# Graph attention on one core: which partitions the two load queues fill when they share a load of the adjacency matrix

## The chip, the cores and the metric

The kernel runs on one core of a Trainium2 chip. The metric is the device time of one execution in microseconds (us), lower is better. Transfers are issued on two queues, one fed by the SyncE sequencer (SP) and one by ScalarE (ACT), and both run on the core's 16 DMA engines.

## The reference

`x` is 4096 x 128, `adj` 4096 x 4096 of int32 with 0 or 1. What is computed:

```
h  = max(layernorm(x), 0)
Wh = h @ W
e  = leaky_relu((Wh @ a1)[:, None] + (Wh @ a2)[None, :], slope 0.2)
e  = where(adj > 0, e, -9e15)
out = x + elu(softmax(e, axis=1) @ Wh)
```

The matrix `adj` is 67.1 MB and is read once; everything else is small.

## The kernel before

The 4096 output rows are worked through in four chunks `c` of 1024 rows. A chunk is made of 8 units `u`, each of 512 columns of `adj`, so that a unit is 1024 rows x 512 columns, 2.1 MB of int32. For a unit ScalarE turns the int32 values to bytes in two activations of 128x2048 elements, TensorE transposes the bytes (16 transposes, line 1017), VectorE multiplies them with the attention weights (line 815, four instructions for a unit, tile `words`), and TensorE multiplies the words with the values (lines 1041 to 1043, tile `acc`).

`adj` comes in 32 loads of 2.1 MB, written out in a table, `LOADS`, and numbered 0 to 31. They land in a ring of four slots, `raw`:

- Loads 0 to 9 are single units; each row of 512 columns is one run of 2 KB. SP fetches both halves (`h is None` below).
- Loads 10 to 19 and 28 to 31 are halves of two neighbouring units: four rows of 1024 columns to each partition, with runs of 4 KB. The text calls these pair loads; `two_to_bytes` (line 554) converts them. In the code they are the entries with a pair of units, and the views `raw_two` and `rows_of_two` belong to them.
- Loads 20 to 27 are sets. They serve the units 4 to 7 of chunks 2 and 3 and come with another layout, in four quarters of 32 partitions each, with runs of 2 KB. VectorE transposes them (line 795, `turn_set`), and `set_to_bytes` (line 572) converts them.

Up to load 11 SP fetches alone (`SHARED` is 12). From load 12 on both queues fetch a part of 1.05 MB each. Of a set SP takes the quarters 0 and 1, that is partitions 0 to 63, and ACT takes 64 to 127. Of a pair load, each queue takes two of the four rows of every one of the 128 partitions. ACT issues its part right after its conversion of the load four before:

```
if at < SHARED: SP alone, k = 0 and 1
SP : raw_two[at % RING][:, 0:2]   <- rows 0, 1 of each partition, to semaphore raw_in[slot][0]
ACT: raw_two[at % RING][:, 2:BT]  <- rows 2, 3 of each partition, to semaphore raw_in[slot][1]
```

The order on each engine is written out by hand. Both queues wait on `act_bytes` until load `at - 4` has been converted. A conversion of a pair load waits for both `raw_in` semaphores of its slot, and of a unit for one per half. Chunk 3 works its units in the order 4, 0, 5, 1, 6, 2, 7, 3: unit 4 wants the sets up to load 27, and unit 0 the pair loads 28 and 29.

Of the kernel before, what the change touches and what calls it, by code (L numbers as in the profile page):

```python
# [16 lines left out]
P = 128  # L17
BT = 4
# [18 lines left out]
RING = 4  # L37
# [5 lines left out]
def bass_graph_attention(nc: bass.Bass, x: bass.AP, adj: bass.AP, w: bass.AP, a: bass.AP, out: bass.AP):  # L43
# [10 lines left out]
    LOADS = [(0, u, None) for u in range(U)] + [(1, u, None) for u in range(2)]  # L54
# [3 lines left out]
    SHARED = U + RING  # L58
# [24 lines left out]
    with ExitStack() as ctx:  # L83
# [6 lines left out]
        def sem(name):  # L90
            return ctx.enter_context(nc.semaphore(name))
# [84 lines left out]
        raw_two = [raw[:, s].rearrange("p (t w) j -> p t (w j)", w=2) for s in range(RING)]  # L176
# [21 lines left out]
        def rows_of(c):  # L198

            if c < SETS:  # L200
                return x_sb[:, group(c)]
            t0 = T * VP // 2 + (c - SETS) * CHUNK
            return val_f32[:, t0:t0 + CHUNK].rearrange("p (t f) -> p t f", f=F)

        def is_set(c, u):
            return c >= SETS and u >= 4
# [14 lines left out]
        def rows_of_two(c, units, h):  # L221

            return (adj_two if c < SETS else adj_two_lin)[c, h, units[0] // 2]
# [6 lines left out]
        raw_in = [[sem(f"raw_in{s}_{k}") for k in range(2)] for s in range(RING)]  # L230
# [76 lines left out]
        gen_out = sem("gen_out")  # L307
        GEN_STEPS = 10
        OUT_DMAS = C - 1 + 3
        SP_QUARTERS, ACT_QUARTERS = (0, 1), (2, 3)  # L310
        MOVES = 4 * 4

        block = ctx.enter_context(nc.Block())
# [8 lines left out]
        @block.sync  # L322
        def _(sp):
            def load_x(b):
                sp.dma_start(x_sb[:, b * BT:(b + 1) * BT, :], x_v[b]).then_inc(x_in[b], 16)

            def load_raw(at, k):
                c, u, h = LOADS[at]
                if h is None:
                    sp.dma_start(raw[:, at % RING, k * BT:(k + 1) * BT], adj_v[c, k, u]).then_inc(raw_in[at % RING][k], 16)  # L330
                else:
                    sp.dma_start(raw_two[at % RING][:, 2 * k:2 * k + 2], rows_of_two(c, u, h)[:, 2 * k:2 * k + 2]).then_inc(raw_in[at % RING][k], 16)

            def load_set(at):

                c, _, h = LOADS[at]
                for k in SP_QUARTERS:
                    sp.dma_start(raw[k * QUARTER:(k + 1) * QUARTER, at % RING], adj_set[c, 1, h, k]).then_inc(set_in[at % RING], 16)

            def load_rows(c):  # L340
                sp.dma_start(rows_of(c).rearrange("p t f -> p (t f)"), x_lin[c]).then_inc(rows_in[c], 16)

            for b in range(4):
                load_x(b)
            load_raw(0, 0)
            for b in range(4, 6):
                load_x(b)
            load_raw(0, 1)
            for b in range(6, NB):
                load_x(b)  # L350
            for at in range(1, C * U):

                if LOADS[at][1] is None:
                    sp.wait_ge(act_bytes, 2 * (at - RING) + 1)
                    load_set(at)
                else:
                    for k in range(2 if at < SHARED else 1):
                        if (at, k) == (RING, 0):
                            sp.wait_ge(first_bytes, 1)
                        elif at >= RING:  # L360
                            sp.wait_ge(act_bytes, 2 * (at - RING) + (k if LOADS[at][2] is None else 1))
                        load_raw(at, k)

            sp.wait_ge(words_free, SETS * U * BT)
            sp.wait_ge(val_moved, MOVES)
            load_rows(C - 2)
            load_rows(C - 1)

            last = out_lin[C - 1].rearrange("p (t f) -> p t f", f=F)
            for k, (t0, t1) in enumerate(BANKS):  # L370
                sp.wait_ge(last_res, k + 1)
                sp.dma_start(last[:, t0:t1], rows_of(C - 1)[:, t0:t1]).then_inc(out_done, 16)

            sp.wait_ge(general_ready, 1)
            with sp.If(sp.value_load(general[0:1, 0:1], min_val=0, max_val=1) > 0):
                sp.wait_ge(out_done, 16 * OUT_DMAS)
                with sp.Fori(0, NB) as b:
                    with sp.Fori(0, BT) as q:
                        sp.wait_ge(gen_res, b * BT + q + 1)
                        sp.nop(nofuse=True)  # L380
                        sp.dma_start(adj_rows, adj_rows_v[bass.ds(b, 1), :, bass.ds(q, 1)].rearrange("g p q j -> (g p q) j")
                                     ).then_inc(gen_in, 16)
                        sp.dma_start(x_tile, x_v[bass.ds(b, 1), :, bass.ds(q, 1)].rearrange("g p q f -> (g p q) f")
                                     ).then_inc(gen_in, 16)
                        sp.wait_ge(gen_res, b * BT + q + 2)
                        sp.nop(nofuse=True)
                        sp.dma_start(out_rows_v[bass.ds(b, 1), :, bass.ds(q, 1)].rearrange("g p q f -> (g p q) f"), res_tile
                                     ).then_inc(gen_out, 16)
                        sp.wait_ge(gen_out, (b * BT + q + 1) * 16)
                        sp.nop(nofuse=True)  # L390

            sp.wait_ge(out_done, 16 * OUT_DMAS)

        @block.gpsimd
        def _(pool):
# [76 lines left out]
            def move_values():  # L472
# [6 lines left out]
                for k in range(4):  # L479
                    for m in range(4):  # L480

                        if moves:
# [3 lines left out]
                                              val_u[m * QUARTER:(m + 1) * QUARTER, (4 + k) * BT:(5 + k) * BT]).then_inc(val_moved, 1)  # L486
                pool.wait_ge(val_moved, MOVES)

# [10 lines left out]
        def _(act):  # L499
# [76 lines left out]
            def load_half(at):  # L576

                if SHARED <= at < C * U:
                    c, u, h = LOADS[at]
                    act.wait_ge(act_bytes, 2 * (at - RING) + 1)  # L580
                    if u is None:
                        for k in ACT_QUARTERS:
                            act.dma_start(raw[k * QUARTER:(k + 1) * QUARTER, at % RING], adj_set[c, 1, h, k]).then_inc(set_in[at % RING], 16)  # L583
                    else:
                        act.dma_start(raw_two[at % RING][:, 2:BT], rows_of_two(c, u, h)[:, 2:BT]).then_inc(raw_in[at % RING][1], 16)

            def row_copy(g, k):
                act.wait_ge(spread_ps, 2 * g + k + 1)
# [8 lines left out]
            def square(g):  # L597

                if g == 0:
                    act.wait_ge(vh_ready, 2 + G - 1)  # L600
                    act.wait_ge(val_moved, MOVES)
                else:
# [58 lines left out]
            for at in range(U, C * U):  # L661
                c, u, h = LOADS[at]
                if u is None:
                    set_to_bytes(c, h)
                elif h is None:
                    for k in range(2):
                        if at == U:
                            row_copy(G - 1, k)
                        to_bytes(c, u, k)
                else:  # L670
                    two_to_bytes(at)
                load_half(at + RING)
                if at == 13:
                    tail(0)
                if at == 27:
                    tail(1)
# [34 lines left out]
        def _(dve):  # L711
# [86 lines left out]
            def weights(c, i, q):  # L798

                n, u = c * U + i, ORDER[c][i]  # L800
                if q == 0:
                    if is_set(c, u):
                        dve.wait_ge(set_turned, (c - SETS) * 4 + u - 4 + 1)
                        dve.wait_ge(val_moved, MOVES)
                    else:
# [165 lines left out]
        def _(pe):  # L971
# [49 lines left out]
            def value_tile(c, i, q):  # L1021
                u = ORDER[c][i]
                return val_set[:, (u - 4) * BT + q] if is_set(c, u) else val[:, u * BT + q]

            def product(c, i, q):
# [3 lines left out]
                if is_set(c, ORDER[c][i]):  # L1029
                    pe.wait_ge(val_moved, MOVES)  # L1030
                v = value_tile(c, i, q)
# [172 lines left out]
```

## Time and profile before

| what | value |
|---|---|
| time, median of 3 runs | 238.54 us (238.23 to 240.66) |
| the profiled execution | 238.26 us, with a span of 236.4 us in the trace and 1.86 us around it |
| TensorE (PE) matmul busy | 218.4 us, 92% of the span |
| VectorE (DVE) busy | 198.7 us, 84% |
| ScalarE (ACT) busy | 158.2 us, 67% |
| GpSimd (POOL) busy | 81.0 us, 34% |
| read from memory | 70.32 MB, 306 GB/s over the span |
| granted TensorE clock | 0.996 of full speed |

The chain of work that ended last is made up of PE for 35% of the span, DMA for 33% and ACT for 17%. Shares of busy time are averages; which engine limits a stretch has to be read stretch by stretch.

### The profile page before, as it was taken

The numbers are of one execution on the slowest core, as the hardware profiler recorded it, in microseconds if no ns is written. First come the engines' busy times: TensorE is split into PE (matmuls) and PEld (weight loads), VectorE is DVE, ScalarE is ACT, GpSimd is POOL, SyncE is SP. The second block draws the span as 40 slices with busy tenths as digits, with TensorE's granted clock in tenths as the row PEclk, the third lists the DMA queues.
The fourth block names the chain that finished last, engine by engine and source line by source line (L and its number), as shares of the span: only waits on it lengthen the run. The fifth ranks groups of instructions, "written<-read, shape, count | busy, mean of one in ns | idle before, by whom it ended". The sixth has DMA issues, their size and how long they took to land.

```text
span 236.4 us, 8053 instructions
## 1 busy us (share of the span) xinstructions
PE 218.4 (92%) x3608; PEld 212.4 (90%) x3608; DVE 198.7 (84%) x266; ACT 158.2 (67%) x139; POOL 81.0 (34%) x68
## 2 busy tenths in 40 slices
PE   6968899999999999999999999999995699999990
PEld 1757899999999999999999999999994699999980
DVE  3999989766669988877787987999989499989866
ACT  3698999966778388977776666666287819920033
POOL 4648127799000110799700300000009700791000
PEclk9999999999999999999999999999999999999998
DMA  6999999999999999999999999999999814010002
GB/s 219 343 392 387 386 386 384 386 385 386 394 408 409 407 409 407 407 411 403 295 316 366 366 362 365 363 362 307 327 407 407 345 70 180 3 79 15 3 0 90
DMA packets 29622, 72.93 MB, mean 308 GB/s; under 512 B 1554, under 2 KB 2068, under 8 KB 29588
## 3 DMA queue, kind: packets, MB, share of 16 engines
q1 hardware_dynamic: 21136, 49.81, 57.6%
q10 hardware_dynamic: 8452, 22.61, 26.4%
q8 instruction: 28, 0.46, 0.8%
q14 instruction: 6, 0.05, 0.1%
HBM read 70.32 MB, written 2.10 MB: 306 GB/s over the span
## 4 chain that ended last, share of the span: by engine, by line
PE 35%; DMA 33%; ACT 17%; DVE 8%; issue 3%; ACTq 2%; DVEq 0%
DMA raw<-in_adj_dram 32%; ACT mask L554 11%; PE acc L1041 10%; PE acc L1043 10%; PE acc L1042 10%; PE mask_t L1017 4%; DVE stats L730 3%; DMA first<-in_x_dram 1%; ACTq L583 1%; PE acc L1005 1%; ACT neg L694 1%; ACT mask L543 1%; DVE wh_sb L756 1%; PE acc L996 1%; ACT second L572 1%
## 5 line engine op out<-in xcount | busy, mean ns | idle before, releaser
L815 DVE SCALAR_TENSOR_TENSOR words<-g_row,gq_word,mask_t 128x1024 f32<-128x1024 f32 x96 | 119.7, 1275 | 27.6 <-PE mask_t L1017 14.7
L1042 PE MATMUL acc<-val,words 128*128 128x129 f16 x744 | 128.0, 220 | 0.0
L1043 PE MATMUL acc<-val,words 128*128 128x129 f16 x744 | 128.0, 220 | 0.0
L1041 PE MATMUL acc<-val,words 128*128 128x129 f16 x744 | 128.0, 220 | 0.0
L1041 PEld LDWEIGHTS acc<-val,words 128*128 128x128 f16 x744 | 72.8, 98 | 0.1
L1042 PEld LDWEIGHTS acc<-val,words 128*128 128x128 f16 x744 | 72.8, 98 | 0.1
L1043 PEld LDWEIGHTS acc<-val,words 128*128 128x128 f16 x744 | 72.8, 98 | 0.0
L554 ACT ACTIVATE mask<-raw,step_bias 128x2048 uint8<-128x2048 int32 x28 | 54.5, 1995 | 19.9 <-DMA raw<-in_adj_dram 7.2
L1041 PE MATMUL acc<-first,words 128*128 128x129 f16 x256 | 43.9, 220 | 2.2 <-DVE num L823 1.6
L1043 PE MATMUL acc<-first,words 128*128 128x129 f16 x256 | 43.9, 220 | 0.0
L1042 PE MATMUL acc<-first,words 128*128 128x129 f16 x256 | 43.9, 220 | 0.0
L815 DVE SCALAR_TENSOR_TENSOR words<-g_row,first,mask_t 128x1024 f32<-128x1024 f32 x32 | 38.7, 1270 | 0.0
L543 ACT ACTIVATE mask<-raw,step_bias 128x2048 uint8<-128x2048 int32 x19 | 37.4, 1997 | 0.6 <-ACT mask L543 0.6
L462 POOL TENSOR_SCALAR hp<-hp 128x1024 f32<-128x1024 f32 x3 | 10.9, 3633 | 69.9 <-ACT neg L649 69.9
L1017 PE MATMUL mask_t<-ident_b,mask 128*128 128x128 bf16 x384 | 25.4, 219 | 3.0 <-ACT mask L554 3.0
L1041 PEld LDWEIGHTS acc<-first,words 128*128 128x128 f16 x256 | 25.0, 98 | 2.5 <-DVE words L815 2.5
L1017 PEld LDWEIGHTS mask_t<-ident_b,mask 128*128 128x128 bf16 x384 | 22.5, 98 | 3.2 <-ACT mask L554 3.1
L1042 PEld LDWEIGHTS acc<-first,words 128*128 128x128 f16 x256 | 25.1, 98 | 0.0
L1043 PEld LDWEIGHTS acc<-first,words 128*128 128x128 f16 x256 | 25.1, 98 | 0.0
L572 ACT ACTIVATE second<-raw,step_bias 128x2048 uint8<-128x2048 int32 x8 | 15.6, 1995 | 7.3 <-DMA raw<-in_adj_dram 7.3
L458 POOL TENSOR_TENSOR hp<-num,rz 128x1024 f32<-128x1024 f32 x3 | 5.7, 1898 | 38.2 <-DVE rz L826 38.1
L572 ACT ACTIVATE g_row<-raw,step_bias 128x2048 uint8<-128x2048 int32 x4 | 8.0, 2004 | 10.2 <-DMA raw<-in_adj_dram 10.2
(113 smaller groups left out, 219.1 us busy)
## 6 DMA issues: line engine op xcount, KB each, us to landing
raw<-in_adj_dram SPq DMA_DIRECT2D x36, 1024.0 KB, 14.6
raw<-in_adj_dram ACTq DMA_DIRECT2D x12, 1024.0 KB, 11.7
raw<-in_adj_dram SPq DMA_DIRECT2D x16, 512.0 KB, 12.4
raw<-in_adj_dram ACTq DMA_DIRECT2D x16, 512.0 KB, 15.6
first<-in_x_dram SPq DMA_DIRECT2D x8, 256.0 KB, 6.5
val<-in_x_dram SPq DMA_DIRECT2D x2, 512.0 KB, 17.0
out_dram<-first ACTq DMA_DIRECT2D x2, 512.0 KB, 3.3
out_dram<-val ACTq DMA_DIRECT2D x1, 512.0 KB, 2.6
```

The source lines that it names most:

```text
L458: nc.gpsimd.tensor_tensor(hp[:], num[:, :, 0:F], rz[:].unsqueeze(2).broadcast_to([P, CT, F]), ALU.mult).then_inc(hp_ready, 1)
L462: nc.gpsimd.tensor_scalar(hp[:], hp[:], 0.0, -1.0, ALU.max, ALU.add).then_inc(pos_ready, 1)
L543: nc.scalar.activation(mask[:, mask_slot(c, u), k * BT:(k + 1) * BT], raw[:, at % RING, k * BT:(k + 1) * BT], ACT.Sign, scale=1.0, bias=st ...
L554: nc.scalar.activation(mask[:, mask_slot(c, u), h * BT:(h + 1) * BT], raw_two[at % RING][:, :, i * BLOCK:(i + 1) * BLOCK], ACT.Sign, scale ...
L572: nc.scalar.activation(pair_bytes[PAIRS[c][k]][:, :, h], raw[:, at % RING, :, k * 256:(k + 1) * 256].rearrange("p t (m x) -> p m t x", m=2 ...
L583: act.dma_start(raw[k * QUARTER:(k + 1) * QUARTER, at % RING], adj_set[c, 1, h, k]).then_inc(set_in[at % RING], 16)
L730: last = nc.vector.bn_stats(stats[:, t, :], x_sb[:, t, :])
L815: nc.vector.scalar_tensor_tensor(words[:, q], g_row[:, c * CHUNK:(c + 1) * CHUNK], word, bytes_t, ALU.max, ALU.mult).then_inc(words_ready, 1)
L1017: last = nc.tensor.transpose(maskt_pairs[:, i % 2, h, t * P:(t + 1) * P], mask_pairs[:, mask_slot(c, u), t, :, h], ident_b[:])
L1041: nc.tensor.matmul(acc_tile(t), high, v[:, 0, 0:V], start=first and t % PT == 0, stop=False, skip_group_check=True)
L1042: nc.tensor.matmul(acc_tile(t), high, v[:, 1, 0:V], start=False, stop=False, skip_group_check=True)
L1043: last = nc.tensor.matmul(acc_tile(t), low, v[:, 0, 0:V], start=False, stop=False, skip_group_check=True)
```

## The change

SP and ACT no longer split a pair load by rows but by partitions, as they do with sets. SP fetches all four rows of partitions 0 to 63, and ACT all four rows of partitions 64 to 127. This holds for the shared pair loads, 12 to 19 and 28 to 31. Loads 10 and 11, which SP fetches alone, stay in two transfers of 128 partitions each. Bytes per transfer, run length, the order of issue, waits and semaphores stay as they are.

```diff
+        SP_HALF, ACT_HALF = slice(0, P // 2), slice(P // 2, P)
...
+            def load_two(at):
+
+                c, u, h = LOADS[at]
+                sp.dma_start(raw_two[at % RING][SP_HALF], rows_of_two(c, u, h)[SP_HALF]).then_inc(raw_in[at % RING][0], 16)
...
-                        load_raw(at, k)
+                        if at < SHARED:
+                            load_raw(at, k)
+                        else:
+                            load_two(at)
...
-                        act.dma_start(raw_two[at % RING][:, 2:BT], rows_of_two(c, u, h)[:, 2:BT]).then_inc(raw_in[at % RING][1], 16)
+                        act.dma_start(raw_two[at % RING][ACT_HALF], rows_of_two(c, u, h)[ACT_HALF]).then_inc(raw_in[at % RING][1], 16)
```

SP's queue from load 2 on, before. The names are the tile and the shape written (partitions x rows x columns); the twelve rows of line 332 are the loads 10 and 11 with two transfers each and 12 to 19 with one:

```order
L330 DMA raw<-in_adj_dram 128x4x512 [waits act_bytes] x11
L332 DMA raw<-in_adj_dram 128x2x1024 [waits act_bytes] x12
L338 DMA raw<-in_adj_dram 32x8x512 [waits act_bytes]
L338 DMA raw<-in_adj_dram 32x8x512
...
L332 DMA raw<-in_adj_dram 128x2x1024 [waits act_bytes] x4
L341 DMA val<-in_x_dram 128x1024 [waits val_moved,words_free]
```

The same place in the changed kernel:

```order
L332 DMA raw<-in_adj_dram 128x4x512 [waits act_bytes] x11
L334 DMA raw<-in_adj_dram 128x2x1024 [waits act_bytes] x4
L339 DMA raw<-in_adj_dram 64x4x1024 [waits act_bytes] x8
L345 DMA raw<-in_adj_dram 32x8x512 [waits act_bytes]
L345 DMA raw<-in_adj_dram 32x8x512
...
L339 DMA raw<-in_adj_dram 64x4x1024 [waits act_bytes] x4
L348 DMA val<-in_x_dram 128x1024 [waits val_moved,words_free]
```

Nothing changed places on SP. Four transfers stay as wide as they were, and twelve are now half as wide and twice as deep.

ACT's queue where the sharing begins, around its parts of loads 12 to 14, before:

```order
L543 ACTIVATE mask<-raw,step_bias 128x2048 [waits turned,raw_in0_1]
L585 DMA raw<-in_adj_dram 128x2x1024 [waits act_bytes]
L543 ACTIVATE mask<-raw,step_bias 128x2048 [waits turned,raw_in1_0]
L543 ACTIVATE mask<-raw,step_bias 128x2048 [waits turned,raw_in1_1]
L585 DMA raw<-in_adj_dram 128x2x1024 [waits act_bytes]
L554 ACTIVATE mask<-raw,step_bias 128x2048 [waits turned,raw_in2_1,raw_in2_0]
```

The same place in the changed kernel:

```order
L553 ACTIVATE mask<-raw,step_bias 128x2048 [waits turned,raw_in0_1]
L595 DMA raw<-in_adj_dram 64x4x1024 [waits act_bytes]
L553 ACTIVATE mask<-raw,step_bias 128x2048 [waits turned,raw_in1_0]
L553 ACTIVATE mask<-raw,step_bias 128x2048 [waits turned,raw_in1_1]
L595 DMA raw<-in_adj_dram 64x4x1024 [waits act_bytes]
L564 ACTIVATE mask<-raw,step_bias 128x2048 [waits turned,raw_in2_1,raw_in2_0]
```

Here too only the shape of the transfers differs. The first such transfer, load 12's part, is issued while SP's queue still holds a load of the old width.

## Rows read from the trace of the kernel before

**Rows 1.** The page: busy tenths of PE and DMA, and GB/s, in 40 slices of 5.9 us

```profile
PE   6968899999999999999999999999995699999990
...
DMA  6999999999999999999999999999999814010002
GB/s 219 343 392 387 386 386 384 386 385 386 394 408 409 407 409 407 407 411 403 295 316 366 366 362 365 363 362 307 327 407 407 345 70 180 3 79 15 3 0 90
```

**Rows 2.** Stretches of the span: us, busy of PE, PEld, DVE, ACT, POOL, clock, DMA share, GB/s

```profile
40.00:64.00 24.00, 24.00 (x409) 23.95 (x407) 16.10 (x14) 18.45 (x15) 16.23 (x10) 1.00 1.05 386
72.00:112.00 40.00, 40.00 (x709) 39.99 (x707) 34.51 (x33) 30.48 (x18) 16.87 (x14) 1.00 1.03 408
113.00:121.00 8.00, 8.00 (x145) 8.00 (x143) 5.56 (x6) 6.36 (x4) 3.90 (x6) 1.00 1.05 279
124.00:160.00 36.00, 36.00 (x640) 36.00 (x638) 32.31 (x30) 25.03 (x14) 1.90 (x1) 1.00 1.06 364
161.00:169.00 8.00, 8.00 (x145) 8.00 (x143) 8.00 (x8) 4.04 (x3) 0.00 (x0) 1.00 1.05 291
170.00:176.00 6.00, 6.00 (x109) 6.00 (x107) 5.14 (x5) 3.93 (x3) 0.00 (x0) 1.00 1.03 406
177.00:186.00 9.00, 3.88 (x64) 3.44 (x62) 6.10 (x8) 7.62 (x6) 8.64 (x4) 1.00 1.02 407
```

**Rows 3.** Waits of PE between 176 and 188 us: total, times, longest

```profile
PE mask_t L1017 <- ACT mask L554: 3.0, 1, 3.0
PE acc L1041 <- DVE num L823: 1.6, 1, 1.6
PE acc L1041 <- DVE words L815: 0.6, 1, 0.6
```

**Rows 4.** ACT in order of time, conversions and issues: start, us, what, idle before

```profile
68.52 0.47 ACTq L585 DMA_DIRECT2D raw<-in_adj_dram  x1
...
73.02 0.47 ACTq L585 DMA_DIRECT2D raw<-in_adj_dram  x1
...
81.09 3.90 ACT L554 ACTIVATE mask<-raw,step_bias 128x2048 uint8<-128x2048 int32 x2 [3.58 <-DMA raw<-in_adj_dram]
...
86.14 3.90 ACT L554 ACTIVATE mask<-raw,step_bias 128x2048 uint8<-128x2048 int32 x2 [1.15 <-DMA raw<-in_adj_dram]
...
128.66 3.90 ACT L572 ACTIVATE second<-raw,step_bias 128x2048 uint8<-128x2048 int32 x2 [1.87 <-DMA raw<-in_adj_dram]
...
134.36 3.90 ACT L572 ACTIVATE second<-raw,step_bias 128x2048 uint8<-128x2048 int32 x2 [1.81 <-DMA raw<-in_adj_dram]
...
145.77 3.90 ACT L572 ACTIVATE second<-raw,step_bias 128x2048 uint8<-128x2048 int32 x2 [1.82 <-DMA raw<-in_adj_dram]
...
163.35 2.00 ACT L572 ACTIVATE g_row<-raw,step_bias 128x2048 uint8<-128x2048 int32 x1 [2.21 <-DMA raw<-in_adj_dram]
...
171.53 2.00 ACT L572 ACTIVATE g_row<-raw,step_bias 128x2048 uint8<-128x2048 int32 x1 [4.28 <-DMA raw<-in_adj_dram]
...
183.25 3.90 ACT L554 ACTIVATE mask<-raw,step_bias 128x2048 uint8<-128x2048 int32 x2 [1.34 <-DMA raw<-in_adj_dram]
```

**Rows 5.** Line 585 between 68 and 69 us: the landing of its one transfer

```profile
DMA to landing us min/median/max: 10.9/10.9/10.9
```

**Rows 6.** DVE in order of time, around unit 4 of chunks 2 and 3

```profile
149.81 1.25 DVE L795 STREAM_TRANSPOSE mask_t<-second 128x1024 uint32<-128x1024 uint32 x1
...
169.80 4.85 DVE L815 SCALAR_TENSOR_TENSOR words<-g_row,first,mask_t 128x1024 f32<-128x1024 f32 x4
175.51 1.26 DVE L795 STREAM_TRANSPOSE mask_t<-g_row 128x1024 uint32<-128x1024 uint32 x1 [0.86 <-issue]
```

**Rows 7.** PE in order of time: the transposes of unit 2 of chunk 1 and of unit 0 of chunk 3

```profile
86.43 1.06 PE L1017 MATMUL mask_t<-ident_b,mask 128*128 128x128 bf16 x16
...
185.31 1.07 PE L1017 MATMUL mask_t<-ident_b,mask 128*128 128x128 bf16 x16 [2.96 <-ACT mask L554]
```

## The prediction

> **What bounds the kernel now.** I read the page's slices first [rows 1]. PE is busy in tenths of 9 from slice 5 to the end, but for two slices near 180 us, and the DMA engines are full from slice 1 to slice 30. So two things run side by side at their limits, and the question is where one waits for the other. The stretches [rows 2] say: PE is busy for the whole of each one up to 176 us and for only 3.88 of 9 us in 177 to 186. The waits of PE there [rows 3] are 3.0 us for a conversion of `mask`, 1.6 us for `num` and 0.6 us for `words`, 5.2 us in all.
>
> The 3.0 us wait ends with the transposes at 185.31 us [rows 7], those of unit 0 of chunk 3. They need the first activation of load 29. Load 29 is the one whose arrival ACT waited for at 183.25 [rows 4]; its two activations take 3.90, so the first ends near 185.25. Only loads 30 and 31 come after it, for units 2 and 3, several units of PE work later. The end of the kernel is therefore the time of these transposes plus a constant, and they have two fetters: the arrival of load 29 plus 2.0 us, and the point where PE itself is through with the work before them, 185.31 - 2.96 = 182.35 us.
>
> Now the loads. The other arrivals that ACT waited for [rows 4] are load 11 at 81.09, load 12 at 86.14, the sets 20, 21 and 23 at 128.66, 134.36 and 145.77, and the sets 26 and 27 at 163.35 and 171.53. Since the engines are full throughout, throughput lost anywhere between 68 and 183 us arrives as lateness of load 29, one to one. The stretches give the rates: units fetched by SP alone 386 GB/s, pair loads 408, sets 364, and two hollows of 8 us with 279 and 291 GB/s [rows 2]. The first hollow ends some 8 us before load 20 arrives, the first set, so it lies where pair loads spread over all partitions meet sets split by partition; the second lies where sets meet pair loads again.
>
> **A reading of the hollows.** If each half of the partitions can take half of the 408 GB/s, 204, then two queues whose bytes fall unevenly on the halves lose. SP spread over all 128 and ACT on 64 to 127 alone, with equal turns, put three quarters of the bytes on the upper half: 204 / 0.75 = 272 GB/s. The hollows have 279 and 291. Sets from both queues are even, and run at 364. The trace doesn't name partitions, so this is an inference; the nearness of 272 to 279 carries it. The Trainium skill (SBUF — State Buffer, section "Door 1: The DMA port swizzle") says the same from the other side: 64 neighbouring partitions reach only 8 of 16 ports. That agrees with the hollows' rates.
>
> **What the change does, part by part.**
>
> *Count of instructions and bytes.* Twelve transfers on each queue change shape; none is added, none moves, all keep 1.05 MB in runs of 4 KB. I cost the issue at nothing: 0.47 us on ACT [rows 4] before as after, and if it rose by a tenth of a microsecond, ACT's waits of 1 to 4 us before its conversions would hide it.
>
> *Edit 1, the start of the sharing: a new hollow.* ACT's part of load 12 is issued at 68.52 [rows 4] and lands 10.9 us later [rows 5], at 79.4, while SP still delivers load 11, 128 partitions wide, until 81.09. Before, the two were alike in width, and no hollow shows (408 in 72 to 112). After, ACT writes the upper half alone beside SP's full width: the pattern of the hollows. At their mean, 285 GB/s, SP's share is 142. How much of SP's wide data lies in the overlap? ACT's part needs 1.05 MB / 204 = 5.1 us, so it began between 68.5 and 74.3, and SP moved for 6.8 to 12.6 us beside it, that is 1.39 to 2.57 MB. I take the 2.1 MB of load 11. At 204 it needs 10.3 us, at 142 it needs 14.8: load 11 is **4.5 us late**, at 85.6; from the bounds 3.0 to 5.5. ACT's parts of 12 and 13 meanwhile run ahead, which gives nothing back: from here SP's parts end each load, and SP can no longer take the whole machine when ACT's queue is empty, since it reaches one half only.
>
> *Edit 2, pair loads 12 to 19 split by partition.* Each needs 1.05 MB of SP. At 204 GB/s that is 5.14 us. The only row with two queues split this way is that of the sets, 364 against 386 for the same 2 KB runs in full width, a factor of 0.94; by it 204 becomes 192, and a load takes 5.46. I take 5.4, close to the row of the same pattern. Eight loads: 43.2 us, to 128.8.
>
> *Edit 3, the two old hollows go.* Pair loads and sets now have the same halves on the same queues. So load 20, a set, follows after its 5.70 us (134.36 - 128.66): at 134.5, **5.8 us later** than the 128.66 of before. Bounds: 84.1 + 8 x 5.14 + 5.7 = 130.9 and 86.6 + 8 x 5.46 + 5.7 = 136.0, late by 2.2 and 7.3. Load 23 stays 17.1 behind load 20, as before: 151.6. Load 27 is 7 x 5.7 = 39.9 behind: 174.4, against 171.53, because the second hollow (8.18 instead of 5.7 us between 26 and 27) is gone. Load 29 is two pair loads on: 185.2, against 183.25, **1.95 us late**.
>
> *The transposes at 185.31.* By load 29: 185.2 + 2.0 = 187.2. By PE's own path: VectorE starts on load 23 at 149.81 with no idle time ahead [rows 6], 0.14 us after its conversion ends (145.77 + 3.90), so its 5.8 us of lateness go straight into VectorE, which then works with little pause (4 words of 1.21 us and a transpose of 1.26 a unit, 8.00 of 8 busy in 161 to 169 [rows 2]) to the transpose at 175.51, where it has 0.86 us idle to give. Load 27's conversion would end at 178.3, which comes before VectorE at 174.65 + 5.8 = 180.45. So PE is ready at 182.35 + 5.8 - 0.86 = 187.3. ACT's own chain, 174.4 + 3.90, two activations of 1.06 with a gap of 0.54, and 3.90 for load 28, ends at 184.9, before load 29. Both paths say 187.3 instead of 185.3: **2.0 us**.
>
> *Where cover could fail.* The lateness of load 11 also meets PE: its transposes at 86.43 [rows 7] need the first activation of load 11, now at 85.6 + 2.0 = 87.6. PE stalls about 1.2 us there. This costs nothing at the end, as PE then waits less at 182 to 187.
>
> **The sum.** Profiled execution: 238.26 = 236.4 + 1.86. With 2.0 more in the span, 238.4 + 1.86 = 240.3 us. The medians of the runs shown lie 0.3 above the profiled execution, which I leave in the range. By the bounds: low, load 29 at 84.1 + 41.1 + 5.7 + 39.9 + 10.3 = 181.1 and PE ready at 182.35 + 2.2 - 0.86 = 183.7, so 1.6 us faster, 236.7; high, PE ready at 188.8 and load 29 at 186.8, so 3.5 slower, 241.8.
>
> **The rivals.**
>
> *A, the old hollows stay as well.* The cause of a hollow may be the switch of the engines from one kind of load to the other, some ahead of others, whichever queue fills which half. For it: the second hollow lasts 8 us, though only four loads are in flight. Then the new hollow is added to two old ones. Each costs 8 us x (386 - 285) GB/s = 0.81 MB, 2.1 us. Load 29 comes at 185.2 + 4.2 = 189.4, the transposes at 191.4: 244.4 us. It decides from the point where load 29's first activation passes PE's own 187.3, so any remainder of a hollow over 0.1 us shows.
>
> *B, no new hollow.* If full width beside the upper half costs nothing when both have 4 KB runs (the hollows mix 4 and 2 KB), load 11 keeps its 81.09, and the old hollows go. Load 29 then comes at 178.1 to 180.7, and PE is ready at 181.5 to 182.8. That is 2.5 to 3.8 us faster: 234.5 to 235.8. Against it: 272 fits the hollows without the run lengths, and the step from 2 to 4 KB runs on SP alone, at 64 to 72 us in the slices, shows no hollow [rows 1].
>
> *C, nothing.* The change does not do what it says for the traffic: engines and turns mix so that width doesn't matter, hollows stay, none is added. 238.3, give or take 0.7.
>
> *D, the halves serialise.* If two half-width transfers took turns, each pair load would need 2.1 MB / 204 = 10.3 us instead of 5.15; ten such loads up to load 29 make 51 us, 289 us. The sets, split this way, run at 364 [rows 2], which is nearly a disproof. The Trainium skill (SBUF — State Buffer, "Can I just issue two DMAs to hit both halves?") holds that two such transfers serialise and gain 6% together; this trace disagrees at 364 GB/s.
>
> **How the numbers follow.** Chances: forecast 0.45, A 0.20, B 0.15, C 0.17, D 0.03. A difference of 1% (236.2 to 240.9) is about what a measurement of this kernel can tell. Faster by over 1%: B and a little of the forecast's low end, 0.17. Within 1%: C and somewhat over half of the forecast, 0.40. Slower: the rest of the forecast, A and D, 0.43. The range takes in the forecast's bounds, C and A, whose own spread ends at 245; it leaves out B below 236.5 and D, together 0.18.
>
> **What would show it.** Right: a hollow of 270 to 300 GB/s between 71 and 87 us; load 11 converted at 85 to 86 instead of 81; a PE stall of about 1 us at its transposes; a flat rate through 112 to 124 and 160 to 169; sets shifted by about 5.8 us; a PE wait near 185 of under 1 us for `mask`. Wrong: 408 GB/s held through 71 to 87 (B); 280 at both old places (A or C); PE waiting at new places in chunk 1 for more than 3 us.

## The result and the profile after

The changed kernel takes 254.71 us (median of 4 runs, 252.16 to 256.29), against 239.34 us for the kernel before beside it. The ratio is 1.060, with a 95% interval of 1.049 to 1.072: slower, and by far more than the forecast of 240.3 us. Medians here take in every run, while ratios and intervals leave out slow ones, over 1.5% above the fastest run of the same kernel. The profiled execution took 252.16 us, with a span of 250.4 us, 14.0 us longer than before.

The page's slices after, answering [rows 1]; here 40 slices of 6.3 us:

```profile
PE   6967999999999999999999995199994499999990
...
PEclk9999999999999999999999999569999889999996
...
GB/s 209 356 389 387 387 386 384 386 385 388 404 346 268 325 334 332 329 336 341 332 310 362 366 365 368 362 361 350 316 323 299 284 158 203 41 3 86 3 0 85
```

PE now has two holes instead of one, and the granted clock falls in or behind both. The rate has a plateau of 325 to 341 GB/s where the pair loads 12 to 19 run, the place that had 408. Stretches of the kernel after, answering [rows 2]; the columns are the same:

```profile
72.00:80.00 8.00, 8.00 (x143) 7.99 (x140) 7.48 (x8) 4.74 (x3) 0.00 (x0) 1.00 1.04 273
88.00:112.00 24.00, 24.00 (x428) 24.00 (x426) 19.52 (x16) 17.59 (x10) 11.02 (x7) 1.00 1.03 332
113.00:121.00 8.00, 8.00 (x145) 8.00 (x143) 5.60 (x5) 3.90 (x2) 7.33 (x11) 1.00 1.03 333
124.00:132.00 8.00, 8.00 (x146) 8.00 (x144) 6.74 (x9) 5.21 (x3) 0.00 (x0) 1.00 1.04 314
136.00:160.00 24.00, 17.72 (x314) 17.54 (x310) 11.94 (x10) 16.29 (x9) 0.00 (x0) 0.94 1.05 365
173.00:181.00 8.00, 8.00 (x145) 8.00 (x143) 8.00 (x8) 3.62 (x2) 0.00 (x0) 1.00 1.03 317
```

The new hollow of 273 GB/s at 72 to 80 us is there, as predicted. Behind it the reader should see what was not predicted: 332 GB/s, steady, for pair loads split by partition. The two old hollows are shallower but still there, later than before: 314 GB/s from 124 to 132 us, behind the issue of the first set's parts at 119.15, and 317 from 173 to 181. The sets run at 365 as before. ACT in order of time, answering [rows 4]:

```profile
82.44 3.90 ACT L564 ACTIVATE mask<-raw,step_bias 128x2048 uint8<-128x2048 int32 x2 [4.99 <-DMA raw<-in_adj_dram]
...
88.55 3.90 ACT L564 ACTIVATE mask<-raw,step_bias 128x2048 uint8<-128x2048 int32 x2 [2.21 <-DMA raw<-in_adj_dram]
...
132.81 3.90 ACT L564 ACTIVATE mask<-raw,step_bias 128x2048 uint8<-128x2048 int32 x2 [1.64 <-DMA raw<-in_adj_dram]
...
138.35 3.90 ACT L582 ACTIVATE second<-raw,step_bias 128x2048 uint8<-128x2048 int32 x2 [1.64 <-DMA raw<-in_adj_dram]
...
155.31 3.89 ACT L582 ACTIVATE second<-raw,step_bias 128x2048 uint8<-128x2048 int32 x2 [1.64 <-DMA raw<-in_adj_dram]
...
172.72 2.00 ACT L582 ACTIVATE g_row<-raw,step_bias 128x2048 uint8<-128x2048 int32 x1 [1.91 <-DMA raw<-in_adj_dram]
...
182.26 2.00 ACT L582 ACTIVATE g_row<-raw,step_bias 128x2048 uint8<-128x2048 int32 x1 [5.64 <-DMA raw<-in_adj_dram]
...
195.57 3.90 ACT L564 ACTIVATE mask<-raw,step_bias 128x2048 uint8<-128x2048 int32 x2 [2.77 <-DMA raw<-in_adj_dram]
```

These are the arrivals of loads 11, 12, 19, 20, 23, 26, 27 and 29. Against [rows 4] the lateness is 1.4 us at load 11, 2.4 at 12, 9.7 at 20, 9.5 at 23, 10.7 at 27 and 12.3 at 29. PE's waits between 148 and 205 us, answering [rows 3], the VectorE row behind the longest, answering [rows 6], and the transposes that wait for load 29, answering [rows 7]:

```profile
PE acc L1051 <- DVE words L825: 8.6, 2, 8.0
PE mask_t L1027 <- ACT mask L564: 4.5, 1, 4.5
PE acc L1051 <- DVE num L833: 1.7, 1, 1.7
```

```profile
159.24 1.26 DVE L805 STREAM_TRANSPOSE mask_t<-second 128x1024 uint32<-128x1024 uint32 x1 [9.64 <-ACT second L582]
```

```profile
197.62 0.56 PE L1027 MATMUL mask_t<-ident_b,mask 128*128 128x128 bf16 x7 [4.55 <-ACT mask L564]
```

The first hole of PE is load 23: its conversion ends at 155.31 + 3.89 = 159.2, VectorE transposes at 159.24 after 9.64 us idle, and PE waits 8.0 us for the words. This wait does not set the end, since PE has to wait for load 29 again. The transposes at 197.62 are 12.3 us later than the 185.31 of before, and the span is 14.0 us longer. The other 1.7 us lie right behind them. The next unit's transposes, before and after, are already 13.95 us apart:

```profile
194.37 1.06 PE L1017 MATMUL mask_t<-ident_b,mask 128*128 128x128 bf16 x16
```

```profile
208.32 1.06 PE L1027 MATMUL mask_t<-ident_b,mask 128*128 128x128 bf16 x16
```

Between the two units the clock was granted at 0.79 from 196 to 204 us, after PE had been idle.

The granted clock (the last column but two) in stretches behind the two holes:

```profile
160.00:164.00 4.00, 2.30 (x22) 2.30 (x23) 4.00 (x5) 2.87 (x2) 0.00 (x0) 0.50 1.06 361
164.00:168.00 4.00, 4.00 (x43) 4.00 (x41) 4.00 (x5) 2.12 (x2) 0.00 (x0) 0.55 1.06 366
168.00:172.00 4.00, 4.00 (x75) 4.00 (x72) 3.87 (x4) 2.81 (x2) 0.00 (x0) 1.00 1.06 361
...
196.00:204.00 8.00, 6.38 (x84) 6.38 (x85) 4.90 (x5) 4.61 (x3) 2.40 (x2) 0.79 0.96 231
```

At 0.55 PE gets through 43 matmuls in 4 us, at 1.00 through 75.

### The profile page after: what moved, and what is told of

Read it like the earlier page. It is cut to its first block, busy times and chain, and to the rows that moved or that the text cites. A ratio compares the mean times of both kernels' runs of the same rounds, so it can differ in the third digit from the quotient of the medians.

```text
span 250.4 us, 8053 instructions
## 1 busy us (share of the span) xinstructions
PE 223.4 (89%) x3608; PEld 217.2 (87%) x3608; DVE 199.1 (80%) x266; ACT 158.2 (63%) x139; POOL 81.1 (32%) x68
## 4 chain that ended last, share of the span: by engine, by line
DMA 36%; PE 34%; ACT 15%; DVE 7%; issue 4%; ACTq 3%; DVEq 0%
DMA raw<-in_adj_dram 35%; PE acc L1051 9%; PE acc L1053 9%; PE acc L1052 9%; ACT mask L564 7%; PE mask_t L1027 4%; DVE stats L740 3%; ACTq L593 2%; ACT mask L553 2%; ACT second L582 2%; DMA first<-in_x_dram 1%; PE acc L1015 1%; ACT neg L704 1%; DVE wh_sb L766 1%; PE acc L1006 1%
## 5 line engine op out<-in xcount | busy, mean ns | idle before, releaser
L1051 PE MATMUL acc<-first,words 128*128 128x129 f16 x256 | 46.7, 227 | 2.2 <-DVE num L833 1.7
L1052 PE MATMUL acc<-first,words 128*128 128x129 f16 x256 | 46.6, 227 | 0.0
L1053 PE MATMUL acc<-first,words 128*128 128x129 f16 x256 | 46.5, 227 | 0.0
L1051 PEld LDWEIGHTS acc<-first,words 128*128 128x128 f16 x256 | 26.1, 102 | 2.6 <-DVE words L825 2.6
L1052 PEld LDWEIGHTS acc<-first,words 128*128 128x128 f16 x256 | 26.1, 102 | 0.0
L1053 PEld LDWEIGHTS acc<-first,words 128*128 128x128 f16 x256 | 26.0, 102 | 0.0
```

The lines of the kernel that those rows point to most:

```text
L1051: nc.tensor.matmul(acc_tile(t), high, v[:, 0, 0:V], start=first and t % PT == 0, stop=False, skip_group_check=True)
L1052: nc.tensor.matmul(acc_tile(t), high, v[:, 1, 0:V], start=False, stop=False, skip_group_check=True)
L1053: last = nc.tensor.matmul(acc_tile(t), low, v[:, 0, 0:V], start=False, stop=False, skip_group_check=True)
```

## The experiments

Each kernel was timed beside the kernel before on the same chip. Most cuts of code leave out the semaphore calls, and where both queues change alike they show one. Rates and arrivals are read from one profiled run of each kernel.

**Source or destination?** The change alters two things in a transfer: which partitions it writes, and which rows it reads. The two queues now read rows megabytes apart. Two kernels take them apart; theory D says that the destination counts (it is not the prediction's rival D), theory S the source. The first keeps full width and reads far apart:

```diff
+    adj_far = adj.rearrange("(c b s p q) (w j) -> c b w s p q j", b=2, s=2, p=P, q=2, j=2 * BLOCK)
-    act.dma_start(raw_two[at % RING][:, 2:BT], rows_of_two(c, u, h)[:, 2:BT])
+    act.dma_start(raw_two[at % RING][:, 2:BT], far(c, u, h, 1))      # SP: far(c, u, h, 0)
```

> The kernel before, with each queue's part of a shared pair load still written over all 128 partitions, but read from two blocks of rows that lie as far apart as in the changed kernel (SP the first half of the rows of a load, ACT the second). Rows so land in other places than the reference wants. Theory D (destination: the halves of the partitions and what they share sets the rate): pair loads stay at 400 to 410 GB/s, time 238 to 240 us. Theory S (source: two far streams of rows clash in memory): pair loads fall to about 333 GB/s as in the changed kernel, time 250 to 255 us.

Measured: ratio 0.995 (0.990 to 0.999), median 238.06 us. Its stretch from 88 to 112 us:

```profile
88.00:112.00 24.00, 24.00 (x428) 24.00 (x426) 19.24 (x16) 19.00 (x11) 17.31 (x16) 1.00 1.03 409
```

409 GB/s: distance in memory costs nothing. The second keeps the halves and reads close together:

```diff
+    adj_near = adj.rearrange("(c b i a s q) (w j) -> c b w s i a q j", b=2, i=P // 2, a=2, s=2, q=2, j=2 * BLOCK)
-    act.dma_start(raw_two[at % RING][ACT_HALF], rows_of_two(c, u, h)[ACT_HALF])
+    act.dma_start(raw_two[at % RING][ACT_HALF].rearrange("p (a q) j -> p a q j", a=2), near(c, u, h, 1))
```

> The changed kernel, with the partitions split 0 to 63 and 64 to 127 as in it, but each queue reads the rows that it read before (two of every four), so the two streams are neighbours in memory again. Rows so land in other places than the reference wants. Theory D: pair loads stay at about 333 GB/s, a hollow of about 270 between 72 and 80 us, time 252 to 256 us. Theory S: 385 to 408 GB/s outside the hollow, time 238 to 242 us.

Measured: ratio 1.059 (1.050 to 1.067), median 253.89 us, the whole slowdown. From 88 to 112 us:

```profile
88.00:112.00 24.00, 24.00 (x428) 24.00 (x426) 18.99 (x15) 16.88 (x11) 8.94 (x4) 1.00 1.03 338
```

The destination decides. Theory S is out.

**Form of the transfer or length of the runs?** Sets also go to halves and yet run at 364. They differ from the changed pair loads in two ways: 32 partitions per transfer, and runs of 2 KB. One kernel takes over each:

```diff
-    sp.dma_start(raw_two[at % RING][SP_HALF], rows_of_two(c, u, h)[SP_HALF])
+    for part in (slice(0, 32), slice(32, 64)):                       # ACT: 64 to 96, 96 to 128
+        sp.dma_start(raw_two[at % RING][part], rows_of_two(c, u, h)[part])
```

> The changed kernel with each queue's part in two transfers of 32 partitions (SP 0 to 31, 32 to 63; ACT 64 to 95, 96 to 127), as sets have them, still in 4 KB runs. If it is the 64-partition form of one transfer that costs the rate, it rises to the sets' 364 GB/s, time 243 to 246 us. If it is the 4 KB runs into a half, or the halves as such, it stays near 333, time 252 to 256 us.

Measured: ratio 1.057 (1.051 to 1.063), median 252.63 us.

```profile
88.00:112.00 24.00, 24.00 (x428) 24.00 (x426) 19.24 (x16) 17.25 (x10) 10.77 (x7) 1.00 1.03 316
```

Quarters in 4 KB runs are no better, 316 GB/s. Now the runs:

```diff
-    sp.dma_start(raw_two[at % RING][SP_HALF], rows_of_two(c, u, h)[SP_HALF])
+    for part in ((SP_HALF, slice(None), slice(0, BLOCK)), (SP_HALF, slice(None), slice(BLOCK, 2 * BLOCK))):
+        sp.dma_start(raw_two[at % RING][part], rows_of_two(c, u, h)[part])      # ACT likewise
```

> The changed kernel with each queue's part in two transfers of 64 partitions x 4 rows x 512 columns, so in 2 KB runs as the sets have. If long runs cost more when two engines want one half, the rate rises to about 364 GB/s, time 243 to 246 us. If the form of 64 partitions sets it, it stays near 333 or falls, by the 0.94 between 386 and 408, to about 315, time 252 to 258 us.

Measured: ratio 1.016 (1.006 to 1.027), median 244.65 us. Stretches of this kernel:

```profile
72.00:80.00 8.00, 8.00 (x143) 7.99 (x141) 7.48 (x8) 6.32 (x4) 0.00 (x0) 1.00 1.05 279
...
88.00:112.00 24.00, 24.00 (x428) 24.00 (x426) 19.25 (x16) 17.27 (x11) 11.84 (x8) 1.00 1.05 361
112.00:124.00 12.00, 12.00 (x216) 12.00 (x214) 9.39 (x9) 8.36 (x5) 7.98 (x12) 1.00 1.05 367
...
160.00:176.00 16.00, 16.00 (x266) 16.00 (x265) 16.00 (x15) 10.12 (x6) 0.00 (x0) 0.93 1.06 355
```

Halving the runs lifts the rate from 332 to 361 GB/s, the sets' own (the quarters are as many transfers, so their number is not it), and both old hollows are gone: the rate stays at 355 to 367 in the stretches from 88 to 176 us. In full width the order is the other way round, 386 with 2 KB runs and 408 with 4 KB [rows 2]. The 386 are SP alone; but SP alone with 4 KB runs moved 411 GB/s from 64 to 68 us of the changed kernel, so that the number of queues does not explain it. The new hollow at 72 to 80, 279 GB/s, stays, for SP's load 11 is still full width beside ACT's upper half.

**Is it the halves, or only that a transfer has 64 partitions?** SP takes the even partitions, ACT the odd ones:

```diff
-        SP_HALF, ACT_HALF = slice(0, P // 2), slice(P // 2, P)
+        SP_HALF, ACT_HALF = slice(0, P, 2), slice(1, P, 2)
```

> The changed kernel with SP taking the even partitions of a shared pair load and ACT the odd ones, so that each queue's part reaches both the lower and the upper 64. Theory D (what counts is which of the lower and upper 64 a queue writes): no hollow at 72 to 80 us, pair loads at 400 to 408 GB/s, old hollows of 280 back at 112 to 120 and 160 to 168, time 238 to 240 us. Rival (fewer partitions in a transfer are slow wherever they lie): 333 GB/s, 252 us.

Measured: ratio 1.002 (0.995 to 1.008), median 239.73 us.

```profile
72.00:80.00 8.00, 8.00 (x142) 7.99 (x140) 7.48 (x8) 6.41 (x4) 0.00 (x0) 1.00 1.03 408
88.00:112.00 24.00, 24.00 (x428) 24.00 (x426) 19.27 (x16) 19.13 (x11) 16.54 (x15) 1.00 1.02 407
113.00:121.00 8.00, 8.00 (x145) 8.00 (x143) 5.56 (x6) 5.18 (x3) 2.35 (x4) 1.00 1.04 273
...
161.00:169.00 8.00, 7.99 (x142) 7.81 (x140) 8.00 (x8) 3.90 (x2) 0.00 (x0) 1.00 1.05 280
```

It behaves like the kernel before in every stretch, the two old hollows included, with 64 partitions, four rows deep, and 4 KB runs in each transfer, as in the changed kernel. So what counts is whether a transfer reaches both the lower and the upper 64.

**The halves tested the other way.** The kernel before, with both queues on the same half in the sets:

```diff
-        SP_QUARTERS, ACT_QUARTERS = (0, 1), (2, 3)
+        SP_QUARTERS, ACT_QUARTERS = (0, 2), (1, 3)
```

> The kernel before with another deal of the sets' quarters: SP 0 and 2, ACT 1 and 3, so both queues write the lower 64 partitions at first and the upper 64 after. Theory D (a half takes about half of the full rate): sets fall from 364 GB/s to between 204 and 300, depending on how far the queues run apart; at 250 the eight sets take 67 us in place of 46, so 20 us more, about 258 us. If halves don't matter: 364 GB/s and 238 us.

Measured: ratio 1.074 (1.057 to 1.091), median 255.67 us.

```profile
124.00:160.00 36.00, 30.81 (x535) 30.13 (x532) 23.50 (x22) 18.58 (x10) 1.90 (x1) 1.00 1.06 257
```

The sets fall from 364 to 257 GB/s. And the changed kernel with everything on SP's queue, lower half, then upper half:

```diff
                 sp.dma_start(raw_two[at % RING][SP_HALF], rows_of_two(c, u, h)[SP_HALF]).then_inc(raw_in[at % RING][0], 16)
+                sp.dma_start(raw_two[at % RING][ACT_HALF], rows_of_two(c, u, h)[ACT_HALF]).then_inc(raw_in[at % RING][1], 16)
-                        act.dma_start(raw_two[at % RING][ACT_HALF], ...)
```

> The changed kernel with ACT's part of each shared pair load issued on SP's queue too, behind SP's own (lower 64, then upper 64, 4 KB runs); ACT issues none of them, sets are as before. If one half can take only half of the full rate, pair loads run at 200 to 220 GB/s and the time is about 290 us, 12 loads x 4.9 us more. If what costs at 333 GB/s is only the meeting of two queues, they run near 408 and the time is 238 to 241 us.

Measured: two runs, 284.64 and 292.04 us; the profile is that of the second.

```profile
88.00:160.00 72.00, 53.85 (x888) 52.79 (x885) 42.79 (x37) 29.39 (x16) 21.69 (x20) 0.95 1.03 219
```

219 GB/s over 72 us is what writing one half at a time gives. The queue itself is not the limit, as SP's 411 GB/s in full width shows. The Trainium skill (SBUF — State Buffer, section "Door 1: The DMA port swizzle") gives about 218 GB/s as the asymptote of partitions 0 to 63, and this row agrees. The same page of the Trainium skill, in "Can I just issue two DMAs to hit both halves?", says that two such transfers together gain 6% over one; the sets' 364 and the changed kernel's 332 GB/s, against 219, disagree with it.

**Which loads cost what.** Only the last four pair loads split, in 4 KB runs:

```diff
-                        if at < SHARED:
+                        if at < 28:
                             load_raw(at, k)
```

> The kernel before, with only the pair loads 28 to 31 split by partition; 12 to 19 stay full width. In the changed kernel load 27 came 9.5 us after load 26 and load 29 another 13.3 after that, where before it was 8.2 and 11.7. If the costs simply add, load 29 comes 2.9 us later than before, near 186.2, and the time is 241 to 242 us. If matched halves do away with the hollow there, as the prediction had it, load 29 comes 1.8 us earlier and the time is 236 to 238 us.

Measured: ratio 1.016 (1.005 to 1.028), median 242.69 us. Loads 27 and 29, and the stretch of the old hollow:

```profile
172.74 2.00 ACT L582 ACTIVATE g_row<-raw,step_bias 128x2048 uint8<-128x2048 int32 x1 [3.99 <-DMA raw<-in_adj_dram]
...
185.43 3.90 ACT L564 ACTIVATE mask<-raw,step_bias 128x2048 uint8<-128x2048 int32 x2 [2.15 <-DMA raw<-in_adj_dram]
```

```profile
161.00:169.00 8.00, 7.75 (x138) 7.58 (x135) 8.00 (x8) 5.62 (x3) 0.00 (x0) 1.00 1.05 340
170.00:176.00 6.00, 5.72 (x101) 5.55 (x99) 6.00 (x6) 3.27 (x2) 0.00 (x0) 1.00 1.03 337
```

The hollow is shallower, 340 in place of 291, but nothing climbs back to 406 behind it. Load 29 is 2.2 us late. Of these, 1.7 us are there at load 24 (153.13 us against 151.46), before the first split load is issued: kernels that are alike up to a load differ by up to 2.7 us in its arrival (load 11: 78.38 us in e6, 81.09 in the kernel before). From load 24 on, the split costs 0.5 us. The span is 5.0 us longer, and the clock accounts for most of the rest: behind PE's 3.9 us wait for load 29 it was granted at 0.50 from 188 to 192 us and at 0.84 to 196, with 40 and 63 matmuls where full clock has 75, which is about 2.5 us.

The counterpart splits only loads 12 to 19 (`at < SHARED or at >= 28` keeps the last four at full width):

> The changed kernel with only the pair loads 12 to 19 split by partition; 28 to 31 are full width again. If the two groups' costs add, the time is that of the changed kernel less what the last four cost alone (1.6%, 3.9 us): 249.5 to 251.5 us, with PE's long wait near 152 us unchanged. If the last four lose more only because the loads before them are late, it falls to 247 or below.

Measured: ratio 1.036 (1.029 to 1.042), median 248.34 us. 3.6% and 1.6% make 5.2%, against 6.0% for both together; with intervals of 0.7 to 1.2 points each that is no evidence against plain addition, nor proof of it. The time lies 1 us under the expected band and above the rival's 247, so this run did not decide between the two. Its profile shows PE's long wait again, 8.9 us, a hollow of 281 GB/s from 172 to 180 us where the full-width pair loads return, and load 29 at 195.30 us, as late as the 195.57 of the changed kernel. As about half of what e7 lost in its profile is the clock, the two ratios are in any case no plain sum of transfer times.

**A version from these findings.** Keep 12 to 19 at full width, where 4 KB runs reach 408; split only 28 to 31 by partition, and in 2 KB runs, so that they match the sets before them in both respects:

```diff
+    for j in (0, BLOCK):                                             # loads 28 to 31 only
+        sp.dma_start(raw_two[at % RING][SP_HALF, :, j:j + BLOCK], rows_of_two(c, u, h)[SP_HALF, :, j:j + BLOCK])
```

> The kernel before, with only the pair loads 28 to 31 split by partition, and each part in two transfers of 64 partitions x 4 rows x 512 columns (2 KB runs). Theory: a hollow needs a queue whose transfers spread over both halves beside one that does not, and long runs into halves are what costs the rest; with neither, the sets' rate runs on. 161 to 169 us at 355 to 360 GB/s in place of 291, load 27 near 169.3 in place of 171.5, load 29 12 to 13 us after it at 181.5 to 182.3 in place of 183.3: 0.5 to 1.5 us faster than before, 237 to 239 us. If the hollow there comes from the change of load kind as such, load 29 comes later than 184 and the time is 240 us or more.

Measured: ratio 0.988 (0.984 to 0.992), median 236.37 us, against 239.62 for the kernel before: faster than both, by a small margin over the kernel before, and under the 237 to 239 expected. Two stretches, the arrival of load 27, and PE's wait for load 29's conversion:

```profile
161.00:169.00 8.00, 7.72 (x137) 7.55 (x135) 8.00 (x8) 5.41 (x3) 0.00 (x0) 1.00 1.06 357
...
177.00:186.00 9.00, 6.13 (x103) 5.64 (x101) 7.19 (x9) 8.68 (x5) 8.76 (x4) 1.00 1.06 358
```

```profile
170.34 2.00 ACT L587 ACTIVATE g_row<-raw,step_bias 128x2048 uint8<-128x2048 int32 x1 [1.91 <-DMA raw<-in_adj_dram]
```

```profile
PE mask_t L1036 <- ACT mask L569: 1.5, 1, 1.5
```

The second hollow is gone, 357 in place of 291 GB/s. Load 27 is converted 17.5 us after load 24 (152.80), in place of 20.1, and load 29 (181.80) 29.0 us after it, in place of 31.8; and PE waits 1.5 us for `mask` in place of 3.0. The profiled spans differ by 1.4 us only, 235.0 against 236.4, the medians by 3.3. The granted clock of the runs beside it was 0.972 to 0.988 for the kernel before and 0.983 to 0.993 here, so a part of the gain may come from shorter waits leaving the clock up; no run takes the two apart.

## Why the prediction was wrong

**The frame held.** The engines are full from 68 us to load 29, lateness adds up to that load, and the end is load 29's first activation plus a constant: 12.3 of the 14.0 us are exactly that. The second path, load 23 through VectorE to PE, showed as well, as the 8.0 us hole. By the prediction's rule it makes PE ready at 182.35 + 9.5 - 0.86 = 191.0 us; it was ready at 197.62 - 4.55 = 193.1, the low clock behind the hole being the likely rest, still ahead of load 29.

**The step that failed is edit 2**, "Pair loads 12 to 19 split by partition". It took the sets' factor of 0.94 for the price of the split. The factor belongs to 2 KB runs (e4: 361 GB/s); with 4 KB runs it is 332 / 408 = 0.81. Eight loads take 132.81 - 82.44 = 50.4 us, 6.3 each, not 43.2. That is 7.2 us of the miss. The row was the only one with that pattern, but it differed in run length, and the prediction's upper bound rested on it too: 5.46 us a load was no bound at all. The sets' own rate, 364 GB/s, gives 5.8 us a load and 46.1 us for eight, close to e4's 47.2 (81.56 to 128.71); the remaining 4.3 us are the 4 KB runs. No row of before showed 4 KB runs into halves, and that gap should have widened the range.

**Edit 1, the new hollow**, was right in place and depth (273 GB/s against 285 taken), and e4 and e5 show its cause: it stays while SP is full width beside ACT's half, and goes when ACT's part reaches both halves. Its size at load 11 can't be judged by the two profiles of the sum, 82.44 against 81.09, 1.4 us where 4.5 were forecast. The 81.09 is the latest of six profiles in which both queues reach both halves there (e5 to e7 and e9 have 78.70, 78.38, 79.45 and 79.64, and e1 78.97 at the latest). With ACT on the upper half it was 82.44, 84.68 (e2) and 82.86 (e10). The means, 79.4 and 83.3, are 4.0 us apart, within the prediction's 3.0 to 5.5. The reading of the hollows took 204 GB/s for a half; with the 219 of e8 it gives 219 / 0.75 = 292, and the hollows had 259 to 291. The stall of PE there did not come in the changed kernel: it was busy for all of 80 to 88 us. The issue, costed at nothing, took ACT 0.56 to 0.67 us in place of 0.47, hidden by its waits as supposed.

**Edit 3, the old hollows go**, was half right. Both came later and shallower, the first at 314 GB/s (124 to 132 us) and the second at 317, and load 27 came 9.5 us after load 26, not 5.7. Matching the halves is not enough: e4, which matches run lengths too, has neither, and e9 lacks the second, the one where its split loads are. Load 29 followed load 27 by 13.3 us instead of 10.8. The step was 11.7 before, 12.7 in e7 with 4 KB runs and 11.5 in e9 with 2 KB, but 13.1 in e4, so the run length explains it in part only, and the rest stays open.

**The transposes.** Forecast 187.3, measured 197.6. Of the 10.3 us between, by arrivals: load 11 was 3.2 earlier than forecast, in part by the late 81.09 that the forecast started from; loads 12 to 19 took 7.2 more; the step to load 20 took 5.54 in place of 5.7; loads 20 to 27 took 4.0 more (43.9 against 39.9), nearly all at the hollow; the last two 2.5 more. That is -3.2 + 7.2 - 0.2 + 4.0 + 2.5 = 10.3.

**Not foreseen: the clock.** Behind the 8.0 us in which PE stood still its granted clock was 0.50, and 196 to 204 us, behind the last wait, ran at 0.79. The prediction put no price on it: "costs nothing at the end" was said of a hole of 1.2 us, and the later one, ahead of unit 0, cost some 1.7 us.

**The rivals.** B is out: a hollow came with 4 KB runs on both sides. A is half right: a hollow between loads of different kind does remain when run lengths differ, at 314 to 317 GB/s instead of 279 to 291. C is out. D is out for two queues, but e8 shows what its rule measures when one queue does both: 219 GB/s, and its 289 us lies between the 284.64 and 292.04 measured.

## What to carry to other kernels

Let every transfer of a bandwidth-bound stream reach both the lower and the upper 64 partitions; if two queues must split by half, keep them on opposite halves, use the same run length on both, and measure the rate for the run length that you will use, since the order of 2 KB and 4 KB runs turns over between full width and halves. A factor read from one pattern may be carried to another only if everything that sets it is the same. Where one kind of load must follow another, making them alike in halves and runs can be worth more than the higher rate of either: e9 gives up 408 for 358 GB/s in four loads and wins 1.2%. And one pair of profiles does not size an effect of 1 or 2 us: load 11 came at 78.4 to 81.1 us in kernels that were alike up to it.

## What the runs showed of the hardware

- One half of the partitions at a time took 219 GB/s (e8), while full width took 408 in the same 4 KB runs: 0.54 of it. Two queues dealt the same half at the same time, in 2 KB runs, had 257 (e6).
- A full-width queue beside one that writes half of the partitions: 259 to 291 GB/s over 8 us (before, after, e2 to e5, e7, e10).
- Two queues on opposite halves: 332 GB/s with 4 KB runs, 361 with 2 KB. Full width: 408 and 386. Why long runs lose there was not tried; two engines meeting at one half for longer is an idea, no more.
- Even and odd partitions, 64 to a transfer, cost nothing (407 GB/s), and neither did streams that lay megabytes apart in memory (409 GB/s).
- After 8.0 us without work TensorE's granted clock was 0.50 of full speed, its lower level of 1.2 GHz, and 1.00 again from 168 us, some 6 us after work had come back. A second idle time of 4.5 us was followed by 0.79 between 196 and 204 us. Waits of about 3 us went both ways: behind 3.0 us in the kernel before the clock stayed at 1.00, behind 2.8 us in e5 it was 0.61 from 184 to 188 us.
